# Attention inside a fused layer: the value products of two steps run back to back in every second step

## The chip, the cores and the metric

One core of a Trainium2 chip. The metric is the device time of one launch in microseconds; of several runs the median counts. Attention is the stretch from 117 to 583 us of the 1096.6 us.

## The reference

For 4 sequences of 1024 tokens with 256 features, one layer of causal attention with 16 heads of 16, and behind it a mixture of 8 experts of which each token takes one. The change touches attention alone:

```python
Q, K, V = (heads(x @ W.T) for W in (Wq, Wk, Wv))   # 16 heads of 16, Q and K rotated by position
logits = einsum('bhnd,bhmd->bhnm', Q, K) * 0.25
logits = where(causal, logits, -inf)
attn = einsum('bhnm,bhmd->bhnd', softmax(logits), V)
x = layernorm(x + attn @ Wo.T)
x = layernorm(x + ffn(x))                          # norm, router, one of 8 experts and a shared one
```

## The kernel before

`attend` works in 16 units, each the 4 heads of one group in one sequence. A unit has 12 steps. Step s takes 128 keys (key tile mt) against the queries of one half of the sequence (chunk c, 512 queries), less those that the causal mask drops: its width is 512 queries or fewer. Five engines run the same list of units and steps, each its own part, and meet by semaphores:

- TensorE, `step` (L993): per step `score(u, s, 0)`, max pieces, `score(u, s, 1)`, max pieces, `times_v` of the step before (L1018), max pieces. `score` multiplies keys and queries of two heads (a pair) into `scores_ps[:, pair]`; there is one such buffer for each pair, so it waits (L957) until the exponential of the step before has read it. `times_v` multiplies the exponentials with the values of the 4 heads, each into 32 columns of the array, in float32 as two halves of four matmuls; it adds into `out_ps` over the steps of a chunk. `turn_out` transposes a finished chunk at s=2 and s=6, `turn_max` the maxima at s=9.
- ScalarE, `exp` (L1029): an exponential for each pair into `probs[:, s % 3]`, after it has waited that the value product which read that buffer is done (L1031); `copy_out` at s=1 and s=5 copies a finished `out_ps`.
- GpSimd, `drop_later_keys` (L1119): zeroes the later keys in steps 0 to 3 and 5 to 8; at s=9 `split_neg` splits the negated maxima, which SP sends into the query stack (L229).
- VectorE: `reduce` of each max piece, `normalise` at s=2 and s=6.

Softmax needs each query's maximum before its scores are formed in full. It is found a unit or two ahead by "max pieces" (`find_max`, L245): 38 in a unit, each up to 512 columns of scores for 1, 2 or 4 heads in one PSUM bank, which VectorE reduces (L301, or L296 with a mask). Three banks go round among the pieces, `turn_out` and `turn_max`; each user waits until the user three before it has been read (`bank_free`, L232).

`attend_plan` (L119) writes the order by hand. A step has three places for pieces: behind pair 0, behind pair 1, behind the value product. Each place has a share of work (L138), and the 38 pieces are dealt out in proportion. Units 14 (from step 8) and 15 have no pieces left; the front part of block 0 of the next stage (`OPEN`, L893) is woven in there. Behind each step stand its width and, in brackets, the pieces in the three places:

| s | 0 | 1 | 2 | 3 | 4 | 5 | 6 | 7 | 8 | 9 | 10 | 11 |
|---|---|---|---|---|---|---|---|---|---|---|---|---|
| width | 512 | 128 | 256 | 384 | 512 | 512 | 384 | 256 | 128 | 512 | 512 | 512 |
| before | 1,2,1 | 0,1,1 | 1,1,0 | 1,1,1 | 1,2,1 | 1,2,1 | 1,1,1 | 1,1,1 | 0,1,0 | 1,2,1 | 1,2,1 | 1,2,1 |
| changed | 1,2,2 | 1,0,0 | 1,1,1 | 1,1,0 | 1,3,1 | 1,2,0 | 1,1,2 | 1,1,0 | 0,1,1 | 1,2,0 | 1,3,1 | 1,2,0 |

The pieces are p0 to p37. A unit's steps 0 to 7 hold p13 to p37 of the next unit, its steps 8 to 11 hold p0 to p12 of the one after that, so p16 is the first behind the value product of s=0.

Of the kernel before, what the change touches and what calls it, by code (L numbers as in the profile page):

```python
# [28 lines left out]
P = 128  # L29
BATCH, SEQ, D = 4, 1024, 256  # L30
# [3 lines left out]
DC = D // P  # L34
BLOCK = 512
BT = BLOCK // P
# [3 lines left out]
GROUP = 4  # L40
# [73 lines left out]


OWN_STEPS = 8


def attend_plan():  # L119

    order = [[0, 3, 2, 1], [0, 4, 5, 6, 7, 1, 2, 3]]
    steps = [(c, mt, max(mt - BT * c, 0) * P) for c in range(2) for mt in order[c]]
    pieces = []
    for t in range(SEQ_TILES):
        for chunk in range(t // BT + 1):
            keys = min((t + 1) * P - chunk * BLOCK, BLOCK)  # L130
            heads = {P: 4, 2 * P: 2}.get(keys, 1)
            pieces += [(h, heads, t, chunk, keys) for h in range(0, GROUP, heads)]


    width = [BLOCK - n0 for _, _, n0 in steps]
    work = []
    for s in range(len(steps)):
        work += [width[s], 2 * width[s], width[s - 1]]  # L138
    until = [round(len(pieces) * d / sum(work)) for d in itertools.accumulate(work)]
    early = len(pieces) - until[3 * OWN_STEPS - 1]  # L140
    places = []
    for begin, end in zip([0] + until, until):
        places.append([(k + early) % len(pieces) for k in range(begin, end)])
    return steps, pieces, places, early
# [438 lines left out]
class Front:  # L583
# [5 lines left out]
    def __init__(self, nc, io, keep, scratch, b):  # L589
# [8 lines left out]
        self.res = b.sb("res", [P, 2, BT, D])  # L598
        self.heads = b.sb("heads_in", [P, 2, BT, GROUPS, GD])
        self.heads_t = b.sb("heads_t", [P, DC, BLOCK])  # L600
        self.x1 = b.sb("x1", [P, 2, BT, D])
        self.xf = b.sb("xf", [P, BT, D])
        self.xf_t = b.sb("xf_t", [P, 2, DC, BLOCK])
        self.row = b.sb("row", [P, 2, BT, RECORD])
        self.stats = b.sb("stats", [P, BT, 6])
        self.moments = b.sb("moments", [P, BT, 2])
# [84 lines left out]
    def route(self, pe, i, batch, odd):  # L691
        nc = self.nc
        pe.wait_ge(self.xf_t_kept, i + 1)
        wait(pe, self.placed, i)
        for t in range(BT):
            for c in range(DC):
                last = nc.tensor.matmul(self.route_ps[:, t * EXPERTS:(t + 1) * EXPERTS],  # L697
                                        self.xf_t[:, odd, c, t * P:(t + 1) * P], self.router[:, c],
                                        start=(c == 0), stop=(c == DC - 1))
        last.then_inc(self.routed, 1)  # L700

# [16 lines left out]
    def keep_xf(self, act, copy, i, batch, odd):  # L718
        act.wait_ge(self.xf_turned, i + 1)
        wait(act, self.up_done, BT * (i - 1))  # L720
        copy(self.xf_t[:, odd], self.front_ps[:]).then_inc(self.xf_t_kept, 1)

    def make_tanh(self, act, i, batch, odd):
        nc = self.nc
# [39 lines left out]
    def norm_first(self, dve, i, batch, odd):  # L764
        nc = self.nc
        dve.wait_ge(self.rstd_made, 2 * i + 1)
        wait(dve, self.added, BT * (i - 1))
        for t in range(BT):
            last = nc.vector.tensor_scalar(self.x1[:, odd, t], self.res[:, odd, t], self.moments[:, t, 0:1],
                                           self.rstd[:, t:t + 1], ALU.subtract, ALU.mult)  # L770
        self.link(dve, i, last)
        self.take_moments(dve, i, self.x1[:, odd])

    def scale_second(self, dve, i, batch, odd):
        nc = self.nc
        dve.wait_ge(self.rstd_made, 2 * i + 2)
        wait(dve, self.row_made, i)
        for t in range(BT):
            last = nc.vector.scalar_tensor_tensor(self.xf[:, t], self.x1[:, odd, t], self.moments[:, t, 0:1], self.ln_w[:],
                                                  ALU.subtract, ALU.mult)  # L780
        self.link(dve, i, last)

# [107 lines left out]
def attend(nc, io, keep, scratch):  # L890
# [8 lines left out]
    k_stack, q_stack, normed = m.k_stack, m.q_stack, m.normed  # L899
    with ExitStack() as ctx:  # L900
        b = Bufs(nc, ctx)
        probs = b.sb("probs", [P, RING, GROUP, BLOCK])
        v_ones = b.sb("v_ones", [P, RING, SEQ_TILES, GROUP, 2 * DK])
        out_t = b.sb("out_t", [P, 2, BLOCK])
        recip = b.sb("recip", [P, 2, BT, GROUP])
# [46 lines left out]
        def _(pe):  # L952
# [13 lines left out]
            def times_v(u, s):  # L966
                if isinstance(u.i, int) and u.i < 0:
                    return
                c, mt, n0 = steps[s]
                if s == 0:  # L970
                    pe.wait_ge(v_grouped, u.i + 1)
                if mt == 0:
                    wait(pe, out_copied, 2 * u.i + c)
                if s in DIAGONAL:
                    pe.wait_ge(masked, len(DIAGONAL) * u.i + DIAGONAL.index(s) + 1)
                else:
                    pe.wait_ge(exp_done, 2 * (STEPS * u.i + s) + 2)
                last_of_chunk = s + 1 == STEPS or steps[s + 1][0] != c
                for h in range(GROUP):
                    last = nc.tensor.matmul(out_ps[32 * h:32 * h + 32, n0:], v_ones[:, u.slot, mt, h],  # L980
                                            probs[:, s % RING, h, n0:], start=(mt == 0), stop=last_of_chunk)
                last.then_inc(pv_done, 1)

            def turn_out(u, c):
# [8 lines left out]
            def step(u):  # L993
                for s in range(STEPS):
                    behind = u if s else u.ahead(-1)
                    ahead = u.ahead(1) if s < OWN_STEPS else u.ahead(2)
                    if s == 2:
                        turn_out(u.ahead(-1), 1)
                    if s == 6:
                        turn_out(u, 0)  # L1000
                    if s == 9:
                        m.turn_max(pe, u.ahead(1))
                    if (u.i, s) == OPEN["turn_heads"]:
                        pe.wait_ge(m.piece_reduced, m.PIECES * UNITS)
                        f.turn_heads(pe, 0, 0, 0)
                    if (u.i, s) == OPEN["turn_xf"]:
                        f.turn_xf(pe, 0, 0, 0)
                    if (u.i, s) == OPEN["route"]:
                        f.route(pe, 0, 0, 0)
                    score(u, s, 0)  # L1010
                    m.find_max(pe, ahead, places[3 * s])
                    score(u, s, 1)
                    m.find_max(pe, ahead, places[3 * s + 1])
                    if (u.i, s) == OPEN["times_wo"]:
                        f.times_wo(pe, 0, 0, 0, range(BT // 2))
                    if (u.i, s) == (OPEN["times_wo"][0], OPEN["times_wo"][1] + 1):
                        f.times_wo(pe, 0, 0, 0, range(BT // 2, BT))
                    times_v(behind, (s - 1) % STEPS)  # L1018
                    m.find_max(pe, ahead, places[3 * s + 2])

            pe.wait_ge(m.k_ones, 1)
            each_unit(step)
            f.count_ranks(pe, 0, 0, 0)
            times_v(Unit.number(UNITS - 1), STEPS - 1)
            turn_out(Unit.number(UNITS - 1), 1)

        @block.scalar
        def _(act):
            def exp(u, s):  # L1029
                c, mt, n0 = steps[s]  # L1030
                wait(act, pv_done, STEPS * u.i + s - 2)  # L1031
                for pair in range(2):
                    act.wait_ge(scores_done, 2 * (STEPS * u.i + s) + pair + 1)
                    nc.scalar.activation(probs[:, s % RING, 2 * pair:2 * pair + 2, n0:],  # L1034
                                         scores_ps[:, pair, :, n0:], ACT.Exp).then_inc(exp_done, 1)

            def copy_out(u, c):
# [67 lines left out]
        def _(pool):  # L1105
# [13 lines left out]
            def drop_later_keys(u, s):  # L1119
# [1 line left out]
                c, mt, n0 = steps[s]  # L1121
                pool.wait_ge(exp_done, 2 * (STEPS * u.i + s) + 2)
                stand(pool, pool_stood)
                tile = probs[:, s % RING, :, n0:n0 + P]
                nc.gpsimd.affine_select(out=tile, in_=tile, compare_op=ALU.is_ge, fill=0.0, base=0,  # L1125
                                        pattern=[[0, GROUP], [1, P]], channel_multiplier=-1).then_inc(masked, 1)

# [28 lines left out]
def feed(nc, io, keep, scratch, out):  # L1156
# [15 lines left out]
    with ExitStack() as ctx:  # L1172
# [44 lines left out]
        gate_done, silu_made, hidden_made = b.sem("gate_done"), b.sem("silu_made"), b.sem("hidden_made")  # L1217
        hidden_turned, hidden_t_kept, down_done = b.sem("hidden_turned"), b.sem("hidden_t_kept"), b.sem("down_done")
        down_in = b.sem("sh_down_in")
        f.front_ps, f.route_ps = front_ps, hidden_ps  # L1220
        block = ctx.enter_context(nc.Block())

# [50 lines left out]
        def _(pe):  # L1273
            def gate(i, n, odd):
                pe.wait_ge(xf_t_kept, i + 1)
                wait(pe, silu_made, IC * i + n - 1)
                for c in range(DC):
                    last = nc.tensor.matmul(gate_ps[:, n % 2], sh_gate[:, c, n * P:(n + 1) * P], xf_t[:, odd, c],  # L1278
                                            start=(c == 0), stop=(c == DC - 1))
                last.then_inc(gate_done, 1)  # L1280

            def up(i, n, odd):
                wait(pe, hidden_made, IC * i + n - 1)
                for c in range(DC):
                    last = nc.tensor.matmul(up_ps[:, n % 2], sh_up[:, c, n * P:(n + 1) * P], xf_t[:, odd, c],  # L1285
                                            start=(c == 0), stop=(c == DC - 1))
                last.then_inc(up_done, 1)

# [177 lines left out]
        def _(dve):  # L1466
# [11 lines left out]
            def add_shared(i, t, odd, batch):  # L1478
                dve.wait_ge(down_done, BT * i + t + 1)
                if t == 0:  # L1480
                    wait(dve, sums_scattered[odd], 16 * BT * batch)
                nc.vector.scalar_tensor_tensor(total[:, odd, t], x1[:, odd, t], 2.0, down_ps[:],  # L1482
                                               ALU.mult, ALU.add).then_inc(added, 1)

            count = [0]
# [241 lines left out]
```

## Time and profile before

| | us |
|---|---|
| median of 3 runs | 1096.91 |
| lowest and highest | 1096.4 and 1099.36 |
| the profiled execution | 1098.5 |
| its span, first to last instruction | 1096.6 |
| TensorE busy | 1023.3 (93%) |
| VectorE busy | 675.0 (62%) |
| ScalarE busy | 457.5 (42%) |
| GpSimd busy | 371.7 (34%) |

PE is TensorE's matmul row, PEld its weight loads, DVE VectorE, ACT ScalarE, POOL GpSimd, SPq the queue that issues DMAs. A matmul's end is modelled and overlaps the next one's start, so for TensorE the starts are read, not the durations: the time from one start to the next is what an instruction takes of the engine. A timeline row puts together instructions of one line that follow each other: the start of the first, the time to the end of the last, and their number.

### The profile page before, as it was taken

How to read it: one execution, taken by the hardware profiler on the slowest of the kernel's cores; microseconds unless marked ns; L12 is line 12 of the kernel's file. 1: busy time of each engine (PE TensorE's matmuls, PEld its weight loads, DVE VectorE, ACT ScalarE, POOL GpSimd, SP SyncE). 2: the span in 40 equal slices, each digit the busy share in tenths (PEclk: the TensorE clock that was granted, in tenths of full speed). 3: DMA queues.
4: the chain of work that ended last, by engine and by line, in shares of the span. 5: the costliest groups of instructions: out<-in, count | busy, mean ns of one | idle time of the engine just before them, and what ended most of it. 6: DMA issues, size and time to landing. Idle time of an engine off the chain costs nothing. (4 is left out here: it accounts for less than half of the span.)

```text
span 1096.6 us, 17525 instructions
## 1 busy us (share of the span) xinstructions
PE 1023.3 (93%) x5522; PEld 534.0 (49%) x5522; DVE 675.0 (62%) x1694; ACT 457.5 (42%) x685; POOL 371.7 (34%) x498
## 2 busy tenths in 40 slices
PE   7998899999997999999998999999977999999995
PEld 4554344444443444444433666666634555555553
DVE  4788888888885888888742555555541333333332
ACT  2552466666764666666664122221111222222221
POOL 7992332222221222222221133333363322233232
PEclk9999899999998999999998999999998999999998
DMA  7786444444446444444004472221522112111211
GB/s 274 188 235 147 65 68 69 70 64 70 69 126 99 64 65 65 62 66 69 11 12 152 136 228 73 74 78 39 194 94 79 59 64 68 62 61 65 67 59 39
DMA packets 78276, 100.06 MB, mean 91 GB/s; under 512 B 28048, under 2 KB 64400, under 8 KB 74864
## 3 DMA queue, kind: packets, MB, share of 16 engines
q1 hardware_dynamic: 63904, 70.48, 31.2%
q0 software_dynamic: 5712, 15.93, 3.8%
q10 hardware_dynamic: 8576, 12.58, 3.4%
q8 instruction: 45, 0.74, 0.3%
q14 instruction: 39, 0.32, 0.1%
HBM read 65.86 MB, written 32.70 MB: 90 GB/s over the span
## 5 line engine op out<-in xcount | busy, mean ns | idle before, releaser
L1034 ACT ACTIVATE probs<-scores_ps 128x1024 f32<-128x1024 f32 (+3 forms) x384 | 290.7, 809 | 140.8 <-PE scores_ps L960 138.8
L301 DVE TENSOR_REDUCE maxima<-max_ps 128x1 f32<-128x512 f32 (+2 forms) x352 | 231.8, 688 | 44.8 <-PE max_ps L259 22.7
L259 PE MATMUL max_ps<-k_stack,q_stack 96*128 96x512 bf16 (+3 forms) x768 | 222.4, 331 | 13.1 <-DMA q_stack<-q_parts 7.0
L1125 POOL TENSOR_SCALAR_AFFINE_SELECT probs<-probs 128x512 f32<-128x512 f32 x128 | 81.7, 638 | 323.4 <-ACT probs L1034 323.4
L960 PE MATMUL scores_ps<-q_stack,k_stack 99*128 99x512 bf16 (+3 forms) x768 | 184.7, 330 | 2.3 <-PEq L359 1.6
L980 PE MATMUL out_ps<-probs,v_ones 128*32 128x512 f32 (+3 forms) x1536 | 164.3, 500 | 2.2 <-POOL probs L1125 1.8
L296 DVE CUSTOM_DVE_ANT_0 masked_out<-max_ps,mask_wide 128x384 bf16<-128x384 f32 (+1 forms) x256 | 151.5, 622 | 20.6 <-PE max_ps L259 18.0
L259 PEld LDWEIGHTS max_ps<-k_stack,q_stack 96*128 96x128 bf16 x768 | 74.6, 97 | 162.3 <-DVE maxima L296 56.5
L1406 ACT ACTIVATE silu<-gate_ps 128x512 f32<-128x512 f32 x71 | 42.4, 597 | 235.1 <-PE gate_ps L1325 138.3
L960 PEld LDWEIGHTS scores_ps<-q_stack,k_stack 99*128 99x128 bf16 x768 | 69.8, 99 | 52.8 <-issue 8.3
L1476 DVE TENSOR_TENSOR hidden<-silu,up_ps 128x512 f32<-128x512 f32 x39 | 26.8, 688 | 104.2 <-PE up_ps L1335 104.2
L1644 POOL DMA_INDIRECT out<-final,target_i x39 | 42.5, 1089 | 112.0 <-DVE final L1574 108.2
L1293 PE MATMUL down_ps<-sh_down_sb,shared_t 128*128 128x256 f32 x256 | 65.3, 399 | 14.8 <-DVE total L1482 9.0
L1325 PE MATMUL gate_ps<-gate_sb,rows_t 128*128 x156 | 75.0, 604 | 0.7 <-issue 0.7
L1335 PE MATMUL up_ps<-up_sb,rows_t 128*128 x156 | 73.4, 593 | 0.0
L1594 POOL DMA_INDIRECT expert_rows<-row,place_i x32 | 31.2, 975 | 116.2 <-DVE place_i L832 93.2
L430 PE MATMUL qk_ps<-x_t,w_qk 128*128 128x512 f32 x128 | 59.5, 618 | 5.5 <-DMA w_qk<-in_Wq 5.5
L1293 PEld LDWEIGHTS down_ps<-sh_down_sb,shared_t 128*128 128x128 f32 x256 | 48.7, 199 | 29.9 <-DVE total L1482 13.2
L1278 PE MATMUL gate_ps<-xf_t,sh_gate_sb 128*128 128x512 f32 x128 | 61.6, 604 | 0.0
L1285 PE MATMUL up_ps<-xf_t,sh_up_sb 128*128 128x512 f32 x128 | 60.3, 593 | 0.2 <-DVE shared_t L1476 0.2
L980 PEld LDWEIGHTS out_ps<-probs,v_ones 128*32 128x32 f32 x1536 | 30.7, 108 | 57.5 <-issue 44.9
L1482 DVE SCALAR_TENSOR_TENSOR total<-x,down_ps 128x256 f32<-128x256 f32 x32 | 13.4, 420 | 59.8 <-PE down_ps L1293 37.5
(169 smaller groups left out, 1272.9 us busy)
## 6 DMA issues: line engine op xcount, KB each, us to landing
k_stack<-k_parts SPq DMA_DIRECT2D x96, 128.0 KB, 4.5
q_stack<-q_parts SPq DMA_DIRECT2D x96, 128.0 KB, 7.5
q_parts<-parts SPq DMA_DIRECT2D x32, 192.0 KB, 3.2
k_parts<-parts SPq DMA_DIRECT2D x32, 192.0 KB, 3.2
rows_in<-expert_rows SPq DMA_DIRECT2D x39, 136.0 KB
sums_in<-expert_sums SPq DMA_DIRECT2D x39, 128.0 KB, 2.0
x_t<-in_x_cols SPq DMA_DIRECT2D x8, 512.0 KB, 10.9
heads_rows<-heads_out SPq DMA_DIRECT2D x32, 128.0 KB, 1.7
```

Source lines behind the costliest of these rows:

```text
L259: last = nc.tensor.matmul(part, self.q_stack[:ROWS, u.slot, h0 + k, t * P:(t + 1) * P], self.k_stack[:ROWS, u.slot, h0 + k, chunk * BLOCK: ...
L296: nc.vector.tensor_tensor_reduce(self.masked_out[:, n % 6, :keys], self.bank("piece", u.i, n)[:, :keys], self.mask_wide[:, BLOCK - keys:], ...
L301: nc.vector.tensor_reduce(self.maxima[:, u.slot, chunk, h0:h0 + heads, t], self.bank("piece", u.i, n)[:, :heads * keys].rearrange("p (h k) ...
L960: last = nc.tensor.matmul(scores_ps[:, pair, k, n0:], k_stack[:ROWS_MAX, u.slot, h, mt * P:(mt + 1) * P], q_stack[:ROWS_MAX, u.slot, h, c ...
L980: last = nc.tensor.matmul(out_ps[32 * h:32 * h + 32, n0:], v_ones[:, u.slot, mt, h], probs[:, s % RING, h, n0:], start=(mt == 0), stop=las ...
L1034: nc.scalar.activation(probs[:, s % RING, 2 * pair:2 * pair + 2, n0:], scores_ps[:, pair, :, n0:], ACT.Exp).then_inc(exp_done, 1)
L1125: nc.gpsimd.affine_select(out=tile, in_=tile, compare_op=ALU.is_ge, fill=0.0, base=0, pattern=[[0, GROUP], [1, P]], channel_multiplier=-1) ...
L1278: last = nc.tensor.matmul(gate_ps[:, n % 2], sh_gate[:, c, n * P:(n + 1) * P], xf_t[:, odd, c], start=(c == 0), stop=(c == DC - 1))
L1285: last = nc.tensor.matmul(up_ps[:, n % 2], sh_up[:, c, n * P:(n + 1) * P], xf_t[:, odd, c], start=(c == 0), stop=(c == DC - 1))
L1293: last = nc.tensor.matmul(down_ps[:], shared_t[:, c, t * P:(t + 1) * P], sh_down[:, c], start=(c == 0), stop=(c == IC - 1))
L1325: last = nc.tensor.matmul(gate_ps[:, j % 2], rows_t[:, j % 2, c * P:(c + 1) * P], gate_w[:, e, c], start=(c == 0), stop=(c == DC - 1))
L1335: last = nc.tensor.matmul(up_ps[:, j % 2], rows_t[:, j % 2, c * P:(c + 1) * P], up_w[:, e, c], start=(c == 0), stop=(c == DC - 1))
```

## The change

Three things in `attend`: (1) the value products of steps s-2 and s-1 are both done in the even step s, and none in odd steps; (2) `probs` gets four buffers, and the exponential waits for the product of four steps back; (3) the pieces are dealt out anew to fit. To make room for the buffer, the odd halves of `x1` and `xf_t` are allocated in the next stage, with the indexing changed from `x1[:, odd, t]` to `x1[odd][:, t]` there. The last unit's products of steps 10 and 11 come behind `count_ranks`.

```diff
+PROBS = 4
@@ attend_plan
-        work += [width[s], 2 * width[s], width[s - 1]]
+        work += [width[s], 2 * width[s], width[s - 2] + width[s - 1] if s % 2 == 0 else 0]
@@ Front.__init__
-        self.x1 = b.sb("x1", [P, 2, BT, D])
+        self.x1 = [b.sb("x1_even", [P, BT, D])]
-        self.xf_t = b.sb("xf_t", [P, 2, DC, BLOCK])
+        self.xf_t = [b.sb("xf_t_even", [P, DC, BLOCK])]
@@ attend
-        probs = b.sb("probs", [P, RING, GROUP, BLOCK])
+        probs = b.sb("probs", [P, PROBS, GROUP, BLOCK])
@@ times_v
-                                            probs[:, s % RING, h, n0:], start=(mt == 0), stop=last_of_chunk)
+                                            probs[:, s % PROBS, h, n0:], start=(mt == 0), stop=last_of_chunk)
@@ step of TensorE
-                    times_v(behind, (s - 1) % STEPS)
+                    if s % 2 == 0:
+                        times_v(behind, (s - 2) % STEPS)
+                        times_v(behind, (s - 1) % STEPS)
                     m.find_max(pe, ahead, places[3 * s + 2])
@@ end of TensorE
             f.count_ranks(pe, 0, 0, 0)
+            times_v(Unit.number(UNITS - 1), STEPS - 2)
             times_v(Unit.number(UNITS - 1), STEPS - 1)
@@ exp of ScalarE
-                wait(act, pv_done, STEPS * u.i + s - 2)
+                wait(act, pv_done, STEPS * u.i + s - PROBS + 1)
@@ feed
+        f.x1.append(b.sb("x1_odd", [P, BT, D]))
+        f.xf_t.append(b.sb("xf_t_odd", [P, DC, BLOCK]))
```

## Rows read from the trace of the kernel before

**Rows 1.** Stretches: length, busy of PE, PEld, DVE, ACT, POOL, clock, DMA.

```profile
381.50:409.80 28.30, 28.30 (x218) 11.85 (x217) 24.85 (x60) 19.38 (x27) 7.01 (x13) 1.00 0.46 67
...
540.00:560.00 20.00, 18.15 (x133) 8.40 (x129) 8.59 (x27) 11.27 (x17) 6.33 (x12) 1.00 0.02 6
```

**Rows 2.** TensorE's timeline, unit 9 step 11: start, length, instructions, [idle before].

```profile
406.98 0.60 PE L960 MATMUL scores_ps<-q_stack,k_stack 99*128 99x512 bf16 x2
407.41 0.38 PE L259 MATMUL max_ps<-k_stack,q_stack 96*128 96x512 bf16 x1
407.63 0.60 PE L960 MATMUL scores_ps<-q_stack,k_stack 99*128 99x512 bf16 x2
408.06 0.59 PE L259 MATMUL max_ps<-k_stack,q_stack 96*128 96x512 bf16 x2
408.59 1.06 PE L980 MATMUL out_ps<-probs,v_ones 128*32 128x512 f32 x8
```

**Rows 3.** Waits of unit 9 (381.5 to 409.8): who for whom, us, times, longest.

```profile
ACT probs L1034 <- PE scores_ps L960: 7.9, 10, 1.7
...
PEld max_ps L259 <- DVE maxima L301: 2.7, 4, 0.8
```

**Rows 4.** Timeline of TensorE: a product of 512 and its second half; one of 128.

```profile
383.32 1.07 PE L980 MATMUL out_ps<-probs,v_ones 128*32 128x512 f32 x8
...
383.78 0.61 PE L980 MATMUL out_ps<-probs,v_ones 128*32 128x512 f32 x4
384.32 0.39 PE L259 MATMUL max_ps<-k_stack,q_stack 96*128 96x512 bf16 x1
...
403.72 0.43 PE L980 MATMUL out_ps<-probs,v_ones 128*32 128x128 f32 x8
404.07 0.34 PE L259 MATMUL max_ps<-k_stack,q_stack 96*128 96x384 bf16 x1
```

**Rows 5.** ScalarE: timeline; groups by shape, 145.5 to 520 (busy, mean ns | idle).

```profile
398.93 1.09 ACT L1034 ACTIVATE probs<-scores_ps 128x512 f32<-128x512 f32 x2 [0.79 <-PE scores_ps L960]
...
407.67 1.94 ACT L1034 ACTIVATE probs<-scores_ps 128x1024 f32<-128x1024 f32 x2 [0.79 <-PE scores_ps L960]
...
L1034 ACT ACTIVATE probs<-scores_ps 128x1024 f32<-128x1024 f32 x154 | 149.4, 1021 | 40.2 <-PE scores_ps L960 38.9
L1034 ACT ACTIVATE probs<-scores_ps 128x512 f32<-128x512 f32 x52 | 28.2, 594 | 31.8 <-PE scores_ps L960 31.8
```

**Rows 6.** Timeline, unit 14 step 11 and unit 15 step 0: no pieces.

```profile
552.01 1.04 PE L960 MATMUL scores_ps<-q_stack,k_stack 99*128 99x512 bf16 x4
...
552.72 3.90 ACT L1034 ACTIVATE probs<-scores_ps 128x1024 f32<-128x1024 f32 x4 [1.76 <-PE scores_ps L960]
...
554.71 0.11 PEld L960 LDWEIGHTS scores_ps<-q_stack,k_stack 99*128 99x128 bf16 x2 [0.62 <-ACT probs L1034]
```

**Rows 7.** Timeline of VectorE, two pieces behind the product of rows 4.

```profile
384.75 1.29 DVE L301 TENSOR_REDUCE maxima<-max_ps 128x1 f32<-128x512 f32 x2 [0.49 <-PE max_ps L259]
```

**Rows 8.** Timeline: exponentials of step 0, their mask, the product that reads it.

```profile
382.16 1.94 ACT L1034 ACTIVATE probs<-scores_ps 128x1024 f32<-128x1024 f32 x2 [0.90 <-PE scores_ps L960]
...
384.26 0.64 POOL L1125 TENSOR_SCALAR_AFFINE_SELECT probs<-probs 128x512 f32<-128x512 f32 x1 [8.11 <-ACT probs L1034]
...
385.14 1.06 PE L980 MATMUL out_ps<-probs,v_ones 128*32 128x512 f32 x8
```

**Rows 9.** Turn of the maxima, SP's three sends (381 to 412), time to landing.

```profile
401.79 0.28 PE L272 MATMUL max_ps<-ident,maxima 128*32 128x128 f32 x1
...
L229 SPq DMA_DIRECT2D q_stack<-neg_parts x3: 513/591/601, 404.5 to 405.7; - x3
...
DMA to landing us min/median/max: 1.8/2.3/2.6
```

**Rows 10.** Waits from 150 to 520 us: the one for a load.

```profile
PE max_ps L259 <- DMA q_stack<-q_parts: 7.0, 1, 7.0
```

More of the change, by code:

```diff
@@ L697, in route @@
                 last = nc.tensor.matmul(self.route_ps[:, t * EXPERTS:(t + 1) * EXPERTS],
-                                        self.xf_t[:, odd, c, t * P:(t + 1) * P], self.router[:, c],
+                                        self.xf_t[odd][:, c, t * P:(t + 1) * P], self.router[:, c],
                                         start=(c == 0), stop=(c == DC - 1))
@@ L720, in keep_xf @@
         wait(act, self.up_done, BT * (i - 1))
-        copy(self.xf_t[:, odd], self.front_ps[:]).then_inc(self.xf_t_kept, 1)
+        copy(self.xf_t[odd][:], self.front_ps[:]).then_inc(self.xf_t_kept, 1)
     def make_tanh(self, act, i, batch, odd):
@@ L768, in norm_first @@
         for t in range(BT):
-            last = nc.vector.tensor_scalar(self.x1[:, odd, t], self.res[:, odd, t], self.moments[:, t, 0:1],
+            last = nc.vector.tensor_scalar(self.x1[odd][:, t], self.res[:, odd, t], self.moments[:, t, 0:1],
                                            self.rstd[:, t:t + 1], ALU.subtract, ALU.mult)
         self.link(dve, i, last)
-        self.take_moments(dve, i, self.x1[:, odd])
+        self.take_moments(dve, i, self.x1[odd])
     def scale_second(self, dve, i, batch, odd):
@@ L778, in scale_second @@
         for t in range(BT):
-            last = nc.vector.scalar_tensor_tensor(self.xf[:, t], self.x1[:, odd, t], self.moments[:, t, 0:1], self.ln_w[:],
+            last = nc.vector.scalar_tensor_tensor(self.xf[:, t], self.x1[odd][:, t], self.moments[:, t, 0:1], self.ln_w[:],
                                                   ALU.subtract, ALU.mult)
@@ L1030, in exp @@
                 c, mt, n0 = steps[s]
-                wait(act, pv_done, STEPS * u.i + s - 2)
+                wait(act, pv_done, STEPS * u.i + s - PROBS + 1)
                 for pair in range(2):
                     act.wait_ge(scores_done, 2 * (STEPS * u.i + s) + pair + 1)
-                    nc.scalar.activation(probs[:, s % RING, 2 * pair:2 * pair + 2, n0:],
+                    nc.scalar.activation(probs[:, s % PROBS, 2 * pair:2 * pair + 2, n0:],
                                          scores_ps[:, pair, :, n0:], ACT.Exp).then_inc(exp_done, 1)
@@ L1123, in drop_later_keys @@
                 stand(pool, pool_stood)
-                tile = probs[:, s % RING, :, n0:n0 + P]
+                tile = probs[:, s % PROBS, :, n0:n0 + P]
                 nc.gpsimd.affine_select(out=tile, in_=tile, compare_op=ALU.is_ge, fill=0.0, base=0,
@@ L1277, in gate @@
                 for c in range(DC):
-                    last = nc.tensor.matmul(gate_ps[:, n % 2], sh_gate[:, c, n * P:(n + 1) * P], xf_t[:, odd, c],
+                    last = nc.tensor.matmul(gate_ps[:, n % 2], sh_gate[:, c, n * P:(n + 1) * P], xf_t[odd][:, c],
                                             start=(c == 0), stop=(c == DC - 1))
@@ L1284, in up @@
                 for c in range(DC):
-                    last = nc.tensor.matmul(up_ps[:, n % 2], sh_up[:, c, n * P:(n + 1) * P], xf_t[:, odd, c],
+                    last = nc.tensor.matmul(up_ps[:, n % 2], sh_up[:, c, n * P:(n + 1) * P], xf_t[odd][:, c],
                                             start=(c == 0), stop=(c == DC - 1))
@@ L1481, in add_shared @@
                     wait(dve, sums_scattered[odd], 16 * BT * batch)
-                nc.vector.scalar_tensor_tensor(total[:, odd, t], x1[:, odd, t], 2.0, down_ps[:],
+                nc.vector.scalar_tensor_tensor(total[:, odd, t], x1[odd][:, t], 2.0, down_ps[:],
                                                ALU.mult, ALU.add).then_inc(added, 1)
```

## The prediction

> **What bounds the kernel now.** I read the table of stretches first. In a unit of attention (28.35 us from one unit's first score product to the next's) TensorE is busy in the whole of it, VectorE in 24.9 us, ScalarE in 19.4 us, GpSimd in 7.0 us [rows 1]. Busy TensorE alone proves little, so the second view is the timeline of TensorE, to see whether a start follows the one before by what the matrix work takes. It does: a score pair 512 wide gives way after 0.43 us, a max piece after 0.22 us, a value product of eight matmuls after 1.00 us, with no hole between [rows 2, 4]. I added these start-to-start times over all of a unit, by columns: score pairs 6 x 0.87 + 2 x 0.65 + 2 x 0.44 + 2 x 0.22 = 7.8 us; 38 max pieces, 24 of 0.22, 8 of 0.17, 4 of 0.34 and 2 of 0.46, 8.9; value products with the way in (below) 10.5; two turns of an output 0.9, that of the maxima 0.1. That makes 28.2 of the 28.35 us. The granted clock is 1.00 of 2.4 GHz [rows 1]. So in 13 of the 16 units TensorE is the bound by its instruction stream, with under 0.2 us of real waiting in a unit. Third, the list of waits: it is ScalarE that waits for scores, ten times in a unit, up to 1.7 us [rows 3]; the other engines have slack on average. What matters is whether they have it at each point of the new order.
>
> **What the change takes away: the way in and out of the 32-column products.** The last two max pieces before a value product start at 408.06 us; 2 x 0.217 later would be 408.49, the product starts at 408.59: 0.09 us for the way in [rows 2]. A product then holds TensorE 1.00 us at 512 columns and 0.35 us at 128 [rows 4]: 0.217 us for each 128 columns and 0.13 us that no column explains. One of the four-matmul halves starts 0.46 us after the product's start (383.78 against 383.32, rows of the same product) and the next engine work 0.54 us after the half (384.32): about 0.09 us of the 0.13 belongs to the way out, the rest to each half [rows 4]. Two products back to back save one way in and one way out: 0.18 us (up to 0.22 if the halves' share goes too, 0 if the seam between two products costs as much as leaving). There are six such pairs in a unit: -1.1 us in a unit (0 to -1.35), -17.4 us over 16 units.
> The Trainium skill, "TensorEngine Tiling (Array Packing)", section Key Properties, says that changing the tiling mode drains TensorE while changing the tile within a mode doesn't. The trace agrees with the 0.09 us on each side; by that rule alone the time would be the profile's 1098.5 less 17.4, about 1081 us.
>
> **What it moves: an odd step has no value product left.** score(s, pair) has to wait until the exponentials of step s-1 of the same pair are done (L957), since scores_ps holds one copy of each pair. Until now a value product stood between the two in every step. Now an odd step is: pair 0, one piece, pair 1, one or two pieces, and then at once pair 0 of the even step. The path over ScalarE: from the start of a 512-wide score pair to its exponential 0.69 us (406.98 to 407.67), the exponential 1.02 us, and 0.05 us to the next start (what is left of the 2.70 us below): 1.77 us [rows 2, 5, 6]. The second exponential comes 0.92 us after the first (1.94 less 1.02), so pair 1 of the next step can't start before 0.69 + 0.92 + 1.02 + 0.05 = 2.68 us, 2.69 unrounded. The trace has this very case where there are no pieces: scores at 552.01, the weights for the second pair of the next step at 554.71 after waiting for ScalarE, 2.70 us later [rows 6]. For other widths the exponential starts 0.26 us after the pair's own 0.11 us for each 128 columns, as 0.69 is 0.43 and 0.26. Against that stands TensorE's own work of an odd step:
> - s=9 (512; pieces of 0.34 + 0.17 + 0.17): 1.54 us of work, wait 0.23; then pair 0 and a piece to 2.37, wait 0.32. Together 0.55.
> - s=11 (512; three pieces of 0.22): 1.52, wait 0.25; then 2.42, wait 0.26. Together 0.51.
> - s=7 (256): first exponential at 0.48, 0.59 long, the second 1.09 - 0.59 = 0.50 behind [rows 5]. Pair 0 of s=8 not before 1.13 against 0.88 of work, pair 1 not before 1.63 against 1.24. Together 0.64.
> - s=3 (384): exponentials 0.81 long and 0.71 apart, halfway between those of 256 and 512 [rows 5]: not before 1.46 against 1.09; then 2.17 against 2.11. Together 0.42.
> - s=5 (512): the turn of the output (0.44) fills the first wait; for pair 1 2.69 against 2.45. 0.23.
> - s=1: the turn of the output fills it, 0.
> The sum is 2.35 us a unit. None of it is covered later: after the two products ScalarE has long caught up and waits itself, so each boundary pays anew.
>
> **The max pieces anew.** Their number is the same. VectorE takes about 0.61 us a piece (1.29 less 0.69 for a second one) and starts 0.43 us after TensorE's start (384.32 to 384.75) [rows 7]; three banks go round. After the two products of s=0 come p16, p17, p18 and then the turn of the output, which takes the bank of p16: that is free 0.43 + 0.69 + 0.06 = 1.18 us after p16's start, the work between is 0.88 us: 0.29 us of wait. p20 then waits some 0.12 us, and p27 (three pieces in a row at s=4) some 0.09 us. Bounds 0 and 0.6; I take 0.4, since the 28.2 of 28.35 us shows that such waits are nearly absent now, and my walk puts them at the two places where three or more pieces now stand together.
> **The fourth buffer** removes no wait that I can find: with three, the exponential of an odd step s waits for the product of step s-3, which is done in the even step before and so ahead of its own scores on TensorE; that of an even step waits for one done two steps before. 0. Splitting x1 and xf_t moves addresses: 0.
> **Masks.** The second product of a pair reads the step just masked. From the last exponential's end (382.16 + 1.94 = 384.10) 0.16 us pass to the mask, which takes 0.64 (384.90), and 0.24 to the product (385.14): 1.04 us [rows 8]; between lies the next score step or the first product, 1.3 us at least. 0; a seam with a mask wait would give back what the pair saves.
> **Queues.** Vector's and GpSimd's orders stay. SP's last send of the negated maxima is issued 3.9 us after the turn of the maxima (401.79 to 405.7) and lands in up to 2.6 us: 6.5 us; the next unit's scores start 8.0 us after it now, 7.2 in my walk [rows 9]. It holds, with 0.6 us to spare; if not, ScalarE and TensorE both stop there. Unit 7 has one wait of 7.0 us for q_stack behind a queue of loads [rows 10]; its start hangs on unit 6's sends, so about 0.6 us of the delay falls into it.
>
> **The sum.** A unit: -1.1 + 2.35 + 0.4 = +1.65 us. Units 0 to 13: +23.1. Unit 7's wait: -0.6. Units 14 and 15: the first half of 14 as the others, +1.3; then no pieces are left and ScalarE sets the pace (3.90 us for four exponentials [rows 6]), two products of 2.0 us stand in the way of scores where one did, but there TensorE waits anyway, for ScalarE and for the front's chain of block 0 (18.15 busy of the 20 us from 540 [rows 1]): +1, between -1 and +5. Together +24.8. The profiled execution took 1098.5 us (span 1096.6); the median is 1096.9. So 1123 in its terms and **1121 us** against the median.
> Against this order the Trainium skill, "TensorE: Matmul & The Clock Gate", section "Step-by-step: what each phase is for", says that matmuls keep their program order and only weight loads are pulled ahead. By that the waiting scores hold everything behind them, as counted here; if products could pass them, the 2.35 us would go and the time be about 1089. No row here shows a passing.
>
> **The rivals**, their times against the median (1.6 us under the profile's).
> 1. Faster: the waits for ScalarE don't bite. Mechanism: TensorE's pieces are held back by the banks in the odd steps anyway, so exponentials finish under that. It decides where an odd step of TensorE lasts 1.77 us without the scores' wait, 0.25 us more than its own work. Then -17.4 us and half the bank waits (3 us): 1083. For it: weight loads of pieces wait for VectorE 2.7 us in a unit [rows 3]; against it: that wait is of the loads, the matmuls follow without a hole, and an odd step begins with banks that VectorE has emptied during the two products. 7%.
> 2. Near nothing: half of the waits, no bank waits: -1.1 + 1.2 a unit, 1098. For it: only that all paths are within 0.3 us of the work. 5%.
> 3. The pair doesn't save (the seam drains, or masks hold it) and the waits come all the same: 17 us more, 1138. For it: the trace has no two products back to back; against it: the two halves within a product follow without a drain. 8%.
> The forecast itself has 80%.
>
> **How the numbers follow.** The forecast's own range is 1110 to 1131 (bank waits 0 to 0.6 a unit: -6 to +3; waits for ScalarE shorter by 0.05 each of nine: -6; the saving between 1.35 and 0.9: -4 to +3; the last two units -2 to +4). To hold 8 in 10 it reaches a bit to both sides: 1107 to 1133. Waits of this size don't lower the clock: 1.00 from 540 to 560 us, where TensorE was busy 18.15 of 20 us [rows 1]. A measurement of this kernel tells about 0.3%, 3.3 us, from nothing: faster 7%, same 5%, slower 88%.
>
> **What the changed profile would show.** TensorE: one pair of products in 2.0 us where two take 2.18; pair 0 of steps 4, 8, 10 and 0 starting 1.77 us (1.46, 1.13) after the pair before; weight loads of scores_ps waiting for ScalarE in every even step, over 30 us in all, where none is listed in a unit now; a unit of 30.0 us instead of 28.35. The forecast is wrong if even steps start with no such wait, if the unit is under 28.3 us, or if the seam shows a gap of 0.18 us.

## The result: 1118.97 us, slower by 1.9%

| | before | changed |
|---|---|---|
| median | 1098.05 us (4 runs) | 1118.97 us (4 runs) |
| lowest, highest | 1096.4, 1099.36 | 1117.9, 1122.43 |
| profiled execution, its span | 1098.5, 1096.6 | 1119.8, 1117.9 |

The ratio is 1.0193, 95% interval 1.0169 to 1.0217. The forecast was 1121 us, range 1107 to 1133.

Step by step, from the first score matmul of one step to that of the next, in unit 9 (worked out from the starts in the two traces; units 1 to 5 and 8 to 13 repeat it within 0.01 us):

| s | 0 | 1 | 2 | 3 | 4 | 5 | 6 | 7 | 8 | 9 | 10 | 11 | unit |
|---|---|---|---|---|---|---|---|---|---|---|---|---|---|
| before | 3.09 | 2.26 | 1.45 | 2.11 | 2.52 | 3.17 | 2.41 | 1.98 | 1.48 | 2.34 | 2.73 | 2.84 | 28.35 |
| changed | 4.34 | 1.29 | 2.66 | 1.45 | 3.27 | 2.16 | 3.48 | 1.16 | 2.82 | 1.77 | 3.49 | 1.86 | 29.74 |

A unit is 1.39 us longer, where 1.65 had been forecast. The same unit in the table of stretches (columns as in [rows 1], which it answers):

```profile
389.61:419.35 29.74, 28.56 (x217) 12.08 (x218) 24.73 (x60) 19.47 (x28) 7.06 (x13) 1.00 0.44 64
```

No engine has more instructions to run; TensorE now has 1.2 us (29.74 less 28.56) in which nothing runs at all. The list of waits of that unit shows what the unit had not before: weight loads of scores waiting for the exponentials, seven times up to 0.6 us. VectorE's waits for max pieces have grown, from 0.5 us to 1.3 us at the longest. The first row below is of the kernel before, the others of the changed one.

```profile
DVE maxima L301 <- PE max_ps L259: 1.2, 3, 0.5
...
ACT probs L1038 <- PE scores_ps L961: 6.0, 5, 1.9
PEld scores_ps L961 <- ACT probs L1038: 3.2, 7, 0.6
...
DVE masked_out L297 <- PE max_ps L260: 2.0, 3, 1.2
...
DVE maxima L302 <- PE max_ps L260: 1.6, 2, 1.3
```

TensorE's timeline around steps 9, 10 and 11 of the changed kernel (start, length, instructions, idle before). It answers [rows 2]:

```profile
412.23 0.60 PE L961 MATMUL scores_ps<-q_stack,k_stack 99*128 99x512 bf16 x2
...
413.00 0.60 PE L961 MATMUL scores_ps<-q_stack,k_stack 99*128 99x512 bf16 x2
413.44 0.49 PE L260 MATMUL max_ps<-k_stack,q_stack 96*128 96x384 bf16 x2
414.00 0.60 PE L961 MATMUL scores_ps<-q_stack,k_stack 99*128 99x512 bf16 x2
414.44 0.33 PE L260 MATMUL max_ps<-k_stack,q_stack 96*128 96x384 bf16 x1
414.92 0.60 PE L961 MATMUL scores_ps<-q_stack,k_stack 99*128 99x512 bf16 x2
...
418.58 0.59 PE L260 MATMUL max_ps<-k_stack,q_stack 96*128 96x512 bf16 x2
419.35 0.38 PE L961 MATMUL scores_ps<-q_stack,k_stack 99*128 99x512 bf16 x1 [0.18 <-ACT probs L1038]
```

Pair 0 of step 9 starts at 412.23, that of step 10 at 414.00: 1.77 us. Two pieces of 384 columns take 0.33 us of TensorE, but from 413.44 to the scores at 414.00 it is 0.56: a wait of 0.23. The piece at 414.44 takes 0.17, the next scores come after 0.48: a wait of 0.31. Both are as forecast (0.23 and 0.32). And the pair of products of step 0, which answers [rows 4]:

```profile
391.65 1.92 PE L981 MATMUL out_ps<-probs,v_ones 128*32 128x512 f32 x16
393.51 0.60 PE L260 MATMUL max_ps<-k_stack,q_stack 96*128 96x512 bf16 x2
```

Sixteen matmuls hold TensorE 1.86 us, where two products held it 1.00 us each and 0.09 for the second way in: 0.23 us less. The seam doesn't drain, which is what "TensorEngine Tiling (Array Packing)" of the Trainium skill says, section Key Properties (a change of tile within a mode needs no drain); the trace agrees.

Where the 21.3 us of the span went, by the same starts: units 1 to 6 and 8 to 13 +16.5, unit 0 +0.3, unit 7 -1.35, unit 14 +3.2, unit 15 up to the first scores of its last step +1.4, the start of attention -0.3, all behind those scores +1.6.

### The profile page after: what moved, and what is told of

The parts are those of the page before. It is cut to its first block and busy times, and to the rows that moved or that the text cites. A ratio compares the mean times of both kernels' runs of the same rounds, so it can differ in the third digit from the quotient of the medians.

```text
span 1117.9 us, 17524 instructions
## 1 busy us (share of the span) xinstructions
PE 1028.3 (92%) x5522; PEld 538.6 (48%) x5522; DVE 672.2 (60%) x1694; ACT 458.9 (41%) x685; POOL 372.8 (33%) x498
## 5 line engine op out<-in xcount | busy, mean ns | idle before, releaser
L302 DVE TENSOR_REDUCE maxima<-max_ps 128x1 f32<-128x512 f32 (+2 forms) x352 | 227.1, 685 | 48.3 <-PE max_ps L260 27.6
L260 PE MATMUL max_ps<-k_stack,q_stack 96*128 96x512 bf16 (+3 forms) x768 | 211.7, 330 | 12.3 <-DMA q_stack<-q_parts 4.5
L961 PE MATMUL scores_ps<-q_stack,k_stack 99*128 99x512 bf16 (+3 forms) x768 | 189.8, 331 | 17.0 <-ACT probs L1038 11.6
L297 DVE CUSTOM_DVE_ANT_0 masked_out<-max_ps,mask_wide 128x384 bf16<-128x384 f32 (+1 forms) x256 | 149.0, 621 | 36.5 <-PE max_ps L260 32.3
L981 PE MATMUL out_ps<-probs,v_ones 128*32 128x512 f32 (+3 forms) x1536 | 147.3, 502 | 0.0
L961 PEld LDWEIGHTS scores_ps<-q_stack,k_stack 99*128 99x128 bf16 x768 | 62.8, 98 | 98.8 <-ACT probs L1038 55.0
L981 PEld LDWEIGHTS out_ps<-probs,v_ones 128*32 128x32 f32 x1536 | 39.9, 110 | 60.3 <-issue 47.4
L1425 ACT COPY rows_t<-front_ps 128x256 f32<-128x256 f32 x39 | 14.5, 373 | 75.8 <-PE front_ps L1320 49.8
L1351 PE MATMUL down_ps<-v_then_down,hidden_t 128*128 x160 | 39.7, 391 | 6.5 <-issue 5.7
L264 PE MATMUL max_ps<-mask,ident_bf 128*128 128x128 bf16 x256 | 43.9, 222 | 0.0
```

The source lines that it names most:

```text
L260: last = nc.tensor.matmul(part, self.q_stack[:ROWS, u.slot, h0 + k, t * P:(t + 1) * P], self.k_stack[:ROWS, u.slot, h0 + k, chunk * BLOCK: ...
L297: nc.vector.tensor_tensor_reduce(self.masked_out[:, n % 6, :keys], self.bank("piece", u.i, n)[:, :keys], self.mask_wide[:, BLOCK - keys:], ...
L302: nc.vector.tensor_reduce(self.maxima[:, u.slot, chunk, h0:h0 + heads, t], self.bank("piece", u.i, n)[:, :heads * keys].rearrange("p (h k) ...
L961: last = nc.tensor.matmul(scores_ps[:, pair, k, n0:], k_stack[:ROWS_MAX, u.slot, h, mt * P:(mt + 1) * P], q_stack[:ROWS_MAX, u.slot, h, c ...
L1351: last = nc.tensor.matmul(slot_down(j), hidden_t[:, j % 2, c * P:(c + 1) * P], down_w[:, e, c], start=(c == 0), stop=(c == IC - 1))
```

## The experiments

A unit's length below is the one that most units of the run repeat, from first scores to first scores. "Waits by the starts" are what a start of TensorE comes later than the columns of the matmul before it and the ways in and out explain; they are worked out for one unit of each trace. In these runs, made on three chips, the kernel before had a median of 1091.4 to 1091.6 us, against which their times stand. Where the time of a version has no interval, it is of a single run.

**Three buffers.** The fourth taken back from the changed kernel:

```diff
-PROBS = 4
+PROBS = 3
```

> The changed kernel with three buffers of exponentials instead of four (the exponential of step s waits for the product of step s-3 again). Theory (the fourth buffer removes no wait): a regular unit stays at 29.74 us, the whole at 1118 to 1121 us. Rival (the pairs need the buffer): an exponential of an odd step waits for the pair of products, 0.3 us or more in each of six odd steps, a unit over 31 us, the whole over 1140 us.

Measured: a unit 29.74 us, every step as in the changed kernel within 0.01 us; one run of 1112.0 us, 1.019 times the kernel before. The fourth buffer does nothing. The halves of `x1` and `xf_t` are still moved here, and no run takes that back alone; the stretch behind attention, where they are used, takes 508.6 to 513.3 us in the seven of these runs that have them moved, and 510.7 to 512.2 in the five that have not, so no cost of it can be seen.

**The old places with the pairs.**

```diff
-        work += [width[s], 2 * width[s], width[s - 2] + width[s - 1] if s % 2 == 0 else 0]
+        work += [width[s], 2 * width[s], width[s - 1]]
```

> The changed kernel with its pairs of products and four buffers, but the max pieces dealt out as in the kernel before, so an odd step keeps the pieces behind its missing product (four pieces at 512 columns instead of three). Theory (the cost is that odd steps have less TensorE work than the 1.77 us that two exponentials need before the next scores): TensorE's own work of an odd 512 step rises from 1.52 to 1.75 us, the waits for ScalarE fall from 2.4 to about 1.1 us a unit (0.21 + 0.28 + 0.41 + 0.08 + 0.06), those for banks stay at 0.4; a unit comes to 28.4 us against 29.74, the whole to 1101 to 1104 us, since the last two units keep their 4 to 5 us. Rival (the pairs cost it by themselves, through the later products and outputs): a unit stays above 29.3 us, the whole above 1113 us.

Measured: 1109.33 us, ratio 1.0159 (1.0123 to 1.0194); a unit 29.55 us. This expectation was wrong by 1.15 us a unit. Half of it came true: the waits for ScalarE nearly went. The waits of the unit from 390.5 us:

```profile
ACT probs L1038 <- PE scores_ps L961: 7.8, 8, 1.6
PEld max_ps L260 <- DVE maxima L297: 3.4, 8, 0.8
PEld max_ps L260 <- DVE maxima L302: 3.0, 6, 0.8
...
DVE masked_out L297 <- PE max_ps L260: 2.3, 3, 1.2
...
PEld scores_ps L961 <- ACT probs L1038: 0.9, 3, 0.4
```

Score loads wait 0.9 us instead of 3.2, but piece loads wait for VectorE 6.4 us (3.4 + 3.0) instead of 2.4 (2.0 + 0.4 in the changed kernel). The loads alone prove little, since in the kernel before they waited 6.2 us (2.7 + 3.5) without a hole between the matmuls. The waits by the starts decide: 2.3 us for banks (1.0 in the changed kernel) and 0.2 us for exponentials (1.8 there). Where TensorE stands still longest, in step 5 of this kernel:

```profile
404.11 0.96 PE L260 MATMUL max_ps<-k_stack,q_stack 96*128 96x384 bf16 x3
405.37 0.63 PE L991 MATMUL max_ps<-ident,out_t 128*128 128x128 f32 x4 [0.30 <-DVE maxima L297]
```

From 404.11 three pieces (0.165 and twice 0.22, 0.60 us of work) take until 405.37, 1.26 us. VectorE is at that time in an unbroken run of reductions, after 0.43 us in which it had no piece behind the pair of step 4. So an odd step is squeezed between two limits: with few pieces it waits for exponentials, with many for VectorE, which ran out of pieces during the pair before.

**The new places without pairs.** The same line, the other way round, in the kernel before.

> The kernel before with one thing of the change: max pieces dealt out as in the changed kernel, products one in each step, three buffers. Theory (the new places only cost because the odd step has no product beside them): a unit 28.4 to 28.7 us, with about 0.1 us of bank waits where three pieces stand in a row, the whole 1098 to 1103 us. Rival (the places are bad by themselves, three and four pieces in a row wait for VectorE's 0.61 us each): a unit over 29 us, the whole over 1108 us.

Measured: 1100.55 us, ratio 1.0084 (1.0055 to 1.0114); a unit 29.00 us, just where the rival's range begins and above the 28.4 to 28.7 expected. With single products in every step the new dealing costs 0.65 us a unit. With pairs it costs 0.19 (29.74 against 29.55): there the two dealings are nearly alike, each for its own reason.

**Single products where no pieces are left.**

```diff
+    PAIRS_UNTIL = (UNITS - 2, 8)
...
-                    if s % 2 == 0:
+                    if (u.i, s) > PAIRS_UNTIL:
+                        times_v(behind, (s - 1) % STEPS)
+                    elif s % 2 == 0:
                         times_v(behind, (s - 2) % STEPS)
                         times_v(behind, (s - 1) % STEPS)
...
-            times_v(Unit.number(UNITS - 1), STEPS - 2)
             times_v(Unit.number(UNITS - 1), STEPS - 1)
```

> The changed kernel, but from step 9 of unit 14 on (where no max pieces are left) products are done one in each step as before. Theory: without pieces ScalarE sets the pace and two products of 1.95 us in a row hold up the next scores; single products give back what units 14 (second half), 15 and the end took, 3 to 5 us: the whole 1114 to 1117 us, units 1 to 13 unchanged at 29.74 us. Rival (the front part of block 0 sets the time there): no change, 1118 to 1121 us.

Measured: 1112.5 us in one run, the three-buffer kernel on the same chip 1112.0. Units 14 and 15 take 58.7 us against its 60.8, up to the first scores of the last step, so 2.2 us come back in attention. What lies behind took 512.4 us here and 508.6 in the other, within the scatter given above. One run can't tell the whole; the 2.2 us are the finding.

**Half of the exponentials**, in both kernels: one head of each pair, read by the products of both. GpSimd then masks half as much too. The output isn't the layer's.

```diff
-                                            probs[:, s % PROBS, h, n0:], start=(mt == 0), stop=last_of_chunk)
+                                            probs[:, s % PROBS, h // 2 * 2, n0:], start=(mt == 0), stop=last_of_chunk)
...
-                    nc.scalar.activation(probs[:, s % PROBS, 2 * pair:2 * pair + 2, n0:],
-                                         scores_ps[:, pair, :, n0:], ACT.Exp)
+                    nc.scalar.activation(probs[:, s % PROBS, 2 * pair, n0:],
+                                         scores_ps[:, pair, 0, n0:], ACT.Exp)
...
```

> The changed kernel with half of ScalarE's exponentials left out: one head of each pair is exponentiated, and the value products of both heads read it, so TensorE's work is the same and the output isn't the layer's. Theory (waits for ScalarE): an exponential takes about 0.59 us at 512 queries, scores can follow after 0.69 + 0.59 + 0.05 = 1.3 us and 1.8 us, both under TensorE's own 1.52 and 2.4; the waits of pair 0 and pair 1 in even steps vanish (2.0 of 2.8 us a unit), a unit comes to 27.5 to 27.9 us, under the 28.35 of the kernel before. Rival (bank waits or the late products make it): a unit stays above 28.8 us.

> The kernel before with the same half of the exponentials left out. Theory: nothing waits for ScalarE there, so a unit stays at 28.3 to 28.35 us; with the changed kernel's 27.5 to 27.9 us this leaves the pairs ahead by 0.5 to 0.9 us a unit once the exponentials are short. Rival: the unit falls by as much as in the changed kernel, 1.8 us or more, and ScalarE was a bound of both.

Measured: changed kernel 28.80 us a unit (1095.5 us), kernel before 28.47 (1089.1 us). The changed kernel's unit is 0.94 us shorter, that of the kernel before 0.11 us longer: ScalarE is a cause, and the pairs' alone. But the changed kernel stays behind, not ahead. The waits for pair 0 and 1 went (step 9 takes 1.53 us, step 11 1.52; by the starts 0.1 us is left for exponentials), and those for banks grew from 1.0 to 1.8 us. Two units are longer, 29.19 and 29.04 us, because the scores that follow them waited for a late send of the negated maxima; the unit behind each is 28.63. The waits of the one from 202.2 us:

```profile
PEld max_ps L260 <- DVE maxima L297: 2.8, 6, 0.8
DVE masked_out L297 <- PE max_ps L260: 2.2, 3, 1.3
...
PEld scores_ps L961 <- DMA q_stack<-neg_parts: 0.7, 1, 0.7
```

**Half of each reduction**, the maxima then being those of half the keys, without and with half of the exponentials:

```diff
-                    self.masked_out[:, n % 6, :keys], self.bank("piece", u.i, n)[:, :keys],
-                    self.mask_wide[:, BLOCK - keys:], 1.0, NEG, ALU.add, ALU.max,
+                    self.masked_out[:, n % 6, :keys // 2], self.bank("piece", u.i, n)[:, :keys // 2],
+                    self.mask_wide[:, BLOCK - keys:BLOCK - keys + keys // 2], 1.0, NEG, ALU.add, ALU.max,
...
-                                    self.bank("piece", u.i, n)[:, :heads * keys].rearrange("p (h k) -> p h k", h=heads),
+                                    self.bank("piece", u.i, n)[:, :heads * keys].rearrange("p (h k) -> p h k", h=heads)[:, :, :keys // 2],
```

> The changed kernel with VectorE's max pieces shortened: each reduces only the first half of its columns, so the maxima are those of half the keys; TensorE's and ScalarE's work is unchanged. Theory (two causes side by side: 1.8 us a unit of waits for exponentials, 1.0 us of waits for banks that VectorE hasn't read): the bank waits go, the others stay: a unit 28.7 to 28.9 us against 29.74. Rival 1 (banks are the whole cause, exponentials only fill the same time): a unit falls to 27.5 us or less. Rival 2 (banks cost nothing of their own): above 29.4 us.

> The changed kernel with half of the exponentials left out (one head of each pair) and half of each max piece's reduction left out. Neither ScalarE nor VectorE can hold TensorE then. Theory (with half the exponentials alone a unit was 28.63 us, since the bank waits took over, 1.66 us): both gone, a unit is 26.9 to 27.2 us, the pure instruction stream with pairs. Rival (something else holds it, the outputs' turns or masks): above 27.6 us.

> The kernel before with the same two halves left out. Theory: neither engine held TensorE there, a unit stays at 28.2 to 28.35 us; the difference to the changed kernel with both halves left out is the pure saving of six pairs, 1.2 to 1.4 us a unit. Rival: it falls below 28.0 us, and the kernel before had waits that the sum of starts hid.

A regular unit, in us:

| left out | before | changed |
|---|---|---|
| nothing | 28.35 | 29.74 |
| half of the exponentials | 28.47 | 28.80 |
| half of the reductions | not run | 29.37 |
| both | 28.35 | 27.40 |

The reductions alone give 0.37 us, at the edge of the second rival (above 29.4), not the 0.9 expected. By the starts the waits for banks fell from 1.0 to 0.1 us, but those for exponentials rose from 1.8 to 2.3. Both halves together give 2.34, 1.03 more than the two singly: each cause covers part of the other's waits. With both left out the pairs are 0.95 us a unit ahead of the kernel before, between the expectation (a unit of 26.9 to 27.2 us) and its rival (above 27.6). Of the 0.44 us that are missing to the 1.39 of six pairs, most is still ScalarE's, since half of an exponential of 256 queries is not short enough: 0.26 us at pair 1 of step 8, as this row names it, and 0.04 each at two more places; 0.1 is left at the turn of step 2.

```profile
267.91 0.11 PEld L961 LDWEIGHTS scores_ps<-q_stack,k_stack 99*128 99x128 bf16 x2 [0.26 <-ACT probs L1038]
```

The kernel before is untouched at 28.35: neither engine held TensorE there.

**The pieces dealt by hand for pairs**, and the same dealing with single products. Counts behind pair 0, pair 1 and the products for each step; the version with pairs also has single products in the last units, by the edit shown above:

```diff
-    width = [BLOCK - n0 for _, _, n0 in steps]
-    work = []
-    ...
+    counts = [[1,2,0],[0,1,1],[1,1,1],[1,1,1],[1,2,1],[1,2,1],[1,1,1],[1,1,1],[1,0,0],[1,2,1],[2,1,1],[1,2,1]]
+    until = list(itertools.accumulate(n for step in counts for n in step))
+    ...
```

> Pairs of products in units 0 to 13 and single products from step 9 of unit 14 on; the pieces dealt by hand so that TensorE has work where it waited: four pieces stay in odd 512 steps, the first piece of the next unit (0.46 us) goes between the two score pairs of step 8, two pieces between those of step 10, and no piece follows the pair of step 0, so that the turn of the output doesn't wait for a bank just filled. Theory: the pair saves 0.23 us (6 a unit, 1.39 us), waits of 0.5 to 0.8 us are left (0.28 of them at the seam of steps 11 and 0): a unit 27.5 to 27.8 us, the whole 1086 to 1093 us, faster than the kernel before by 0.5 to 1%. Rival (VectorE at 24.9 us of busy time a unit can't follow the pieces so bunched): bank waits grow to over 1.4 us, a unit 28.3 us or more, the whole 1097 us or more.

> The kernel before, single products, with the pieces dealt as in the hand-dealt version with pairs. Theory: single products leave nothing for the dealing to fill, a unit stays at 28.3 to 28.5 us, the whole at 1096 to 1100 us, so a gain of the hand-dealt version comes from its pairs. Rival: the dealing is better by itself and takes the kernel below 1094 us.

Measured: with pairs 1109.22 us, ratio 1.0176 (1.0155 to 1.0198), a unit 29.62 us: the rival, by a wide margin. With single products 1094.02 us, ratio 1.0032 (1.0016 to 1.0048), a unit 28.62, a little over the 28.5 expected. The waits of a unit with pairs:

```profile
PEld max_ps L258 <- DVE maxima L295: 3.4, 8, 0.8
...
DVE masked_out L295 <- PE max_ps L258: 2.4, 3, 1.2
PEld max_ps L258 <- DVE maxima L300: 2.4, 6, 0.6
...
PEld scores_ps L960 <- ACT probs L1038: 0.7, 2, 0.4
```

Again ScalarE's share is gone and VectorE's is there: 0.1 and 2.5 us by the starts. Three dealings, whose odd steps of 512 hold 3 or 4 pieces, give 29.55 to 29.74 us; that no other dealing does better with six pairs and three banks isn't shown.

**One pair only**, the products of steps 2 and 3 in step 4, in the kernel before:

```diff
-                    times_v(behind, (s - 1) % STEPS)
+                    if s == 4:
+                        times_v(behind, s - 2)
+                    if s != 3:
+                        times_v(behind, (s - 1) % STEPS)
```

> The kernel before with a single pair of products, that of steps 2 and 3 (256 and 384 columns, 1.22 us together) in step 4; pieces and the three buffers of exponentials as before. Theory (a pair pays where it is short and the step before it keeps its pieces): in the changed order with the old places steps 3 and 4 took 1.46 + 3.02 = 4.48 us against 4.63 before, so a unit comes to 28.15 to 28.25 us, 0.1 to 0.2 us less, the whole about 2 us (0.2%) faster. Rival (VectorE pays it back in step 5, whose pieces and turn of the output come behind): a unit 28.35 us or more, no gain.

Measured: 1090.39 us (12 runs) against 1091.61 (17 runs), ratio 0.9986 (0.9973 to 0.9999); a unit 28.20 us, steps 3 and 4 together 4.48 against 4.63. A pair of 640 columns in all, after a step that keeps its three pieces, pays 0.15 us of its 0.23. It is the fastest version here that gives the layer's output, by 1.2 us, where about 2 were expected.

```profile
386.39 0.60 PE L960 MATMUL scores_ps<-q_stack,k_stack 99*128 99x512 bf16 x2
386.83 0.38 PE L259 MATMUL max_ps<-k_stack,q_stack 96*128 96x512 bf16 x1
387.09 0.60 PE L960 MATMUL scores_ps<-q_stack,k_stack 99*128 99x512 bf16 x2
387.53 0.55 PE L259 MATMUL max_ps<-k_stack,q_stack 96*128 96x512 bf16 x2
388.01 1.28 PE L980 MATMUL out_ps<-probs,v_ones 128*32 128x256 f32 x16
```

Step 4 of it: from the scores at 386.39 to the next at 387.09 it is 0.70 us against 0.65 of work, so 0.05 us of wait is all that is left there. The changed kernel has 0.04 at the same place, after a wait of 0.36 at pair 0, which is gone here.

## Why the prediction was right, and where not

- **The bound** (TensorE's stream, 28.2 of 28.35 us): right. With both halves left out the kernel before has the same 28.35 us. The 2.7 us of piece loads that the first rival cites are only those behind one line; [rows 3] leaves out 3.5 us more, 6.2 in all, and neither held a matmul.
- **The ways in and out** (-1.1 us a unit, up to -1.35): the term was too small. A pair of 512 columns saves 0.23 us, six 1.39; the halves' share goes too, and the saving lies just beyond the upper end taken.
- **The waits for exponentials** (2.35 us): in the places forecast. Steps 3, 7, 9 and 11 take 1.45, 1.16, 1.77 and 1.86 us where 1.46, 1.13, 1.77 and 1.77 stood. By the starts of unit 9 they are 1.8 us, since in step 5 and at pair 0 of step 8 waits for banks came first. With half of the reductions left out, when next to no bank was waited for, they were 2.3 us, and step 7 took 1.13: the size was right, and what was missed is that the banks take a part of it. Pair 0 after step 11 waits 0.09 longer than worked out, in every unit; the sends of the maxima aren't it, since the last of them lands anywhere from 0.07 to 1.6 us before the load while the 0.09 stays the same. What it is stays open.
- **The waits for banks** (0.4, bounds 0 to 0.6): too small, and outside the bounds: 1.0 us by the same starts, of it 0.38 before the turn of the output at s=2 (0.29 forecast), 0.09 before p27 (as forecast), 0.22 in step 5 before the other turn and 0.27 in step 7 before p37. The last two stand in no line of the forecast; those for p20 (0.12 forecast) didn't come. Both kinds together are 2.8 us where 2.75 stood. The split was off and the sum held, in part because the two take each other's time; that it held to 0.03 us is luck. So "none of it is covered later" was wrong in that form. It held for the time, not for what a remedy would give: leaving half of the exponentials out returned 0.94 us, not 1.8.
- **What follows from it** was therefore misjudged in the expectations of the runs: that the dealing of the pieces costs the time, and that better places would turn the pairs into a gain. Three dealings show otherwise. Behind the two longest pairs, in steps 0 and 6, VectorE stands idle for 1.35 and 1.25 us, behind the shorter ones for up to 0.45. In the changed kernel, step 0:

```profile
393.93 1.89 DVE L302 TENSOR_REDUCE maxima<-max_ps 128x1 f32<-128x512 f32 x3 [1.35 <-PE max_ps L260]
```

  Three banks hold 1.9 us of its work and are read by then, and it lacks that time afterwards: before the change it had 24.9 us of work in a unit of 28.35 and wasn't the idle engine that its 62% of the whole span shows.
- **The fourth buffer, masks, queues**: 0 for the buffer is shown by the run with three. All six pairs of unit 9 pass from one product to the next without a gap, so no mask held a seam. The negated maxima came in time, but not with 0.6 us to spare: the 2.6 us to landing were read over one unit, and at the start of the unit from 204.98 us the last send landed 7.1 us after the turn, 0.07 us before the scores' weights were loaded. With half of the exponentials left out they came too late twice.
- **Unit 7** (-0.6): -2.7 (8.9 us over a regular unit before, 6.2 after). The wait for the load fell from 7.0 [rows 10] to 4.5 us:

```profile
PE max_ps L260 <- DMA q_stack<-q_parts: 4.5, 1, 4.5
```

  In two further runs of the same order, with three buffers and with single products at the end, unit 7 took 37.8 and 36.8 us instead of 35.9. So what goes beyond the forecast is about as large as the scatter from run to run.
- **The last units** (+2.3 for units 14 and 15): +4.6; single products there bring 2.2 back. Behind attention, where 0 stood, 1.6 us more were measured, less than the 4.7 us by which that stretch differs between the other runs.
- Of the rivals, the faster one had a part of the mechanism: in steps 5 and 7 of the changed kernel, and in most odd steps of the old dealing, banks do hold the pieces back and cover ScalarE. But they cost the same time, so there was no gain. The second fell with waits of 2.8 us a unit where it had 1.2. The third fell with the seam of 0 us.

Over the whole, the regular units cost 5 us less than forecast, unit 7 2 us less, and the end 4 us more: the span grew by 21.3 us where 24.8 stood. The medians are nearer, 1119 and 1121, because the median before rose by 1.1 us with its fourth run. That the misses have both signs and nearly cancel is luck; the mechanism (pairs save TensorE time, odd steps pay more in waits) is not.

## What to carry to other kernels

Before work is moved out of a step, work out the shortest time between two uses of each single buffer (start of the matmul, its reader, back again: here 1.77 us) and check that each step still holds that much; that ScalarE was busy for 19 us in 28 says nothing on it. Work put together in one place leaves its neighbours without work for as long as it lasts: ask what each other engine has stored by then, here three banks against 1.9 us. Two waits that fall into the same stretch hide each other, so an experiment that removes one gives its share only after the other is gone; run both, singly and together.

## What the runs showed of the hardware

Eight float32 matmuls of 32 columns cost TensorE their columns, 0.09 us on the way in, 0.09 on the way out and some 0.02 at each half; across the seam of a pair the way in and out and the share of the halves all vanish (1.86 us against 2.09). In both kernels regular units repeat to 0.01 us over eleven of them. They do so between runs whose whole time differs: the changed order takes 29.74 us in its own trace and in two of the further ones, where the kernels ran 0.6% faster as a whole, and the kernel before and its version with both halves left out both take 28.353 us. So a single trace tells 0.1 us in a unit, 0.13% of the kernel, where the times of single runs of one kernel on one chip spread over 0.3 to 0.7%.
